# One 32x32 TensorE tile per head for state times queries, two PSUM banks for the attention output, no block-diagonal state, and a new program order

## The reference

```python
x = x + 0.5 * ffn(layernorm(x))
x = x + retention_layer(layernorm(x))
x = x + 0.5 * ffn(layernorm(x))

def ffn(x):                         # x_prev: x shifted by one token
    xr = mu_r * x + (1.0 - mu_r) * x_prev
    xk = mu_k * x + (1.0 - mu_k) * x_prev
    return sigmoid(xr @ W_r.T) * (square(relu(xk @ W_k.T)) @ W_v.T)

def step(S, (qc, kc, vc)):          # 8 heads of 32 channels, one chunk of tokens
    attn = einsum('bhid,bhjd->bhij', qc, kc) * D
    o_intra = einsum('bhij,bhje->bhie', attn, vc)
    o_inter = einsum('bhid,bhde->bhie', qc * decay_q, S)
    S_new = decay_s * S + einsum('bhjd,bhje->bhde', kc * decay_k, vc)
    return S_new, o_intra + o_inter
```

## Time and profile before

| | |
|---|---|
| median of 3 runs | 348.6 us (348.55 to 348.75) |
| the profiled execution's own time | 348.72 us |
| its span in the trace | 346.8 us |
| TensorE busy | 325.5 us (94%) |
| VectorE busy | 302.0 us (87%) |
| ScalarE busy | 211.3 us (61%) |
| GpSimd busy | 161.3 us (47%) |

### The profile page before, as it was taken

How to read it: one execution, slowest core, us unless ns; L and a number is a source line. 1 busy time by engine, 2 the same in 40 slices (tenths; PEclk the granted TensorE clock), 3 DMA queues, 4 the chain that set the end, 5 groups by cost and what they waited for, 6 DMA issues and landing times.

```text
span 346.8 us, 10332 instructions
## 1 busy us (share of the span) xinstructions
PE 325.5 (94%) x3861; PEld 312.9 (90%) x3861; DVE 302.0 (87%) x693; ACT 211.3 (61%) x418; POOL 161.3 (47%) x270
## 2 busy tenths in 40 slices
PE   0869999899999999999999999999999999999874
PEld 0759999899999999999999999999999999999864
DVE  3898997999899998989899898989999897898843
ACT  3675557567657657657757757656766657455352
POOL 4384463435627282644727183563736171414140
PEclk9999999999999999999999999999999999999999
DMA  7611010000101020200202020110000000000001
GB/s 259 221 30 28 9 32 2 33 2 10 54 3 62 2 62 2 62 3 2 62 3 62 2 61 2 22 43 32 3 4 30 2 32 2 33 2 32 33 0 60
DMA packets 11664, 12.15 MB, mean 35 GB/s; under 512 B 992, under 2 KB 11232, under 8 KB 11616
## 3 DMA queue, kind: packets, MB, share of 16 engines
q1 hardware_dynamic: 11328, 11.44, 10.4%
q10 hardware_dynamic: 288, 0.07, 0.1%
HBM read 7.31 MB, written 4.19 MB: 33 GB/s over the span
## 4 chain that ended last, share of the span: by engine, by line
PE 84%; DVE 8%; issue 3%; ACT 2%; POOL 1%; DMA 1%; DVEq 0%; ACTq 0%; POOLq 0%
PE bank L903 36%; PE bank L895 24%; PE bank L887 6%; PE bank L973 5%; PE bank L987 5%; PE bank L1000 4%; PE bank L963 2%; PE bank L1010 2%; DVE stats L524 1%; DMA x<-in_x 1%; DVE xrT L551 1%; DVE xk_lo L556 1%; DVE dT L535 1%; DVE xkT L544 1%; ACT xn L294 1%
## 5 line engine op out<-in xcount | busy, mean ns | idle before, releaser
L213 POOL TENSOR_TENSOR xr_lo<-xrT,xr_hi 128x512 fp32r<-128x512 f32 x32 | 54.3, 1697 | 95.0 <-ACT xr_hi L314 93.7
L294 ACT ACTIVATE xn<-x,shift,rstd 128x256 f32<-128x256 f32 x96 | 52.2, 593 | 12.7 <-POOL shift L209 12.7
L222 POOL TENSOR_TENSOR state_bd<-state,mask 128x256 f32<-128x256 f32 x31 | 27.8, 898 | 39.2 <-DVE state L620 37.2
L606 DVE TENSOR_TENSOR attn<-bank,decay 128x512 f32<-128x512 f32 x64 | 40.4, 677 | 1.0 <-PE bank L973 0.6
L895 PE MATMUL bank<-xk_hi,w_hi 128*128 128x256 f32 x128 | 38.3, 299 | 1.9 <-DVE xk_lo L556 1.9
L903 PE MATMUL bank<-w_hi,xr_hi 128*128 128x256 f32 x128 | 39.0, 305 | 0.5 <-POOL xr_lo L213 0.4
L524 DVE BATCH_NORM_STATS2 stats<-x 128x6 f32<-128x256 f32 x96 | 35.7, 413 | 4.2 <-DMA x<-in_x 4.0
L903 PE MATMUL bank<-w_hi,ka_hi 128*128 128x256 f32 x128 | 36.5, 285 | 2.8 <-DVE ka_lo L562 2.8
L887 PE MATMUL bank<-ident,xn 128*128 128x128 f32 x192 | 30.0, 280 | 9.7 <-ACT xn L294 9.7
L202 POOL TENSOR_TENSOR var_eps<-moments,eps 128x2 f32<-128x2 f32 x48 | 20.6, 428 | 38.3 <-DVE moments L528 38.1
L895 PE MATMUL bank<-xa_hi,w_hi 128*128 128x256 f32 x128 | 36.8, 287 | 0.0
(11 more groups left out here) (80 smaller groups left out, 1071.2 us busy)
## 6 DMA issues: line engine op xcount, KB each, us to landing
x<-in_x SPq DMA_DIRECT2D x16, 256.0 KB, 3.0
x_out<-y SPq DMA_DIRECT2D x16, 256.0 KB, 2.6
w_f<-in_w SPq DMA_DIRECT2D x7, 256.0 KB, 5.4
decay<-in_decay SPq DMA_DIRECT2D x1, 512.0 KB, 6.4
decq<-in_decq SPq DMA_DIRECT2D x1, 256.0 KB, 6.0
deck<-in_deck SPq DMA_DIRECT2D x1, 256.0 KB, 6.1
mask<-in_mask SPq DMA_DIRECT2D x1, 128.0 KB, 5.7
ident<-in_ident ACTq DMA_DIRECT2D x1, 64.0 KB, 2.6
```

Source lines behind the costliest of these rows:

```text
L213: pool.tensor_tensor(xr_lo[f][n % 2][:], xrT[f][n % 2][:], xr_hi[f][n % 2][:].bitcast(F32), ALU.subtract).then_inc(xr_lo_ready[f], 1)
L222: pool.tensor_tensor(state_bd[1 - c][:], state[c][:].unsqueeze(2).broadcast_to([P, G, HG, HD]), mask[:], ALU.mult).then_inc(state_bd_ready ...
L294: act.activation(xn[s][n % 2][:, t, :], x[n % len(x)][:, t, :], ACT.Identity, bias=shift[s][n % 2][:, t:t + 1], scale=rstd[s][n % 2][:, t: ...
L606: dve.tensor_tensor(attn[r][:], bank[B_SCORES[r]][:].rearrange("p (g c i) -> p g c i", g=G, c=TILES), decay[:, r, :, :].unsqueeze(2).broad ...
```

## The change

The product of state and queries is done by 16 matmuls per block, one for each head and chunk, each with 32 rows and 32 columns of the array and 128 columns of queries. They read `state_dec`, which DVE writes in any case. `state_bd`, `mask`, its DMA and POOL's `spread_state` go away. Both chunks are now done in one call, `inter(n)`, and so are those of `outer(n)`. Head `r` of group `g` uses array columns and output partitions `(r + g) % 4`, and each group has a PSUM bank of its own (banks 3 and 4). The rows of Wo are permuted on the host to fit. As `inter` now reads the decayed state of both chunks, it waits for `state_scaled[0]` and `state_scaled[1]`, and DVE's chain from `outer` through `update_state(0)` and `scale_state(1)` stands ahead of it. The banks of nearly everything else are given out anew, and the order of the calls is new on all four engines, with some work moved: the high parts of W_R, W_O and W_VAL are made by POOL, the low part of W_K by DVE. At the start there are 8 and 10 matmuls of keep_warm, in the epilogue none.

```diff
@@ TensorE helpers
-            def inter(c, n):
-                if c == 0:
-                    pe.wait_ge(q_ready, n + 1)
-                    pe.wait_ge(state_bd_ready[0], n)
-                    if n == 0:
-                        pe.wait_ge(state_zeroed, 2)
-                else:
-                    pe.wait_ge(state_bd_ready[1], n + 1)
-                for g in range(G):
-                    mm = pe.matmul(halves(B_OT)[:, g, c * P:(c + 1) * P], state_bd[c][:, g, :, :].rearrange("p h e -> p (h e)"),
-                                   qT[:, g, c * P:(c + 1) * P], start=(c == 0 and g == 0), stop=(c == 1),
-                                   skip_group_check=True)
-                mm.then_inc(inter_done[c], 1)
+            def quadrant(g, r):
+
+                q = (r + g) % HG
+                return slice(q * HD, (q + 1) * HD)
+
+            def inter(n, first=False):
+
+                pe.wait_ge(q_ready, n + 1)
+                for c in range(TILES):
+                    pe.wait_ge(state_scaled[c], n + 1)
+                for c in range(TILES):
+                    for g in range(G):
+                        for r in range(HG):
+                            rows = slice(r * HD, (r + 1) * HD)
+                            mm = pe.matmul(bank[B_OT + g][quadrant(g, r), c * P:(c + 1) * P], state_dec[c][rows, g, :],
+                                           qT[rows, g, c * P:(c + 1) * P], start=(first and c == 0), stop=(not first and c == 1),
+                                           skip_group_check=True)
+                mm.then_inc(inter_done, 1)
@@ POOL
-            def spread_state(c, n):
...
-                pool.wait_ge(state_ready[c], n + 1)
-                pool.wait_ge(inter_done[1 - c], n + c)
-                pool.tensor_tensor(state_bd[1 - c][:], state[c][:].unsqueeze(2).broadcast_to([P, G, HG, HD]),
-                                   mask[:], ALU.mult).then_inc(state_bd_ready[1 - c], 1)
...
             inverse_std(FFN1, 0)
-            split_low(pool, W_K)
+            split_high(pool, W_R)
             inverse_std(FFN1, 1)
@@ TensorE, start
             transpose_T(FFN1, 0)
             pe.wait_ge(w_hi_ready[W_K], 1)
-            keep_warm(3, 8)
+            keep_warm(4, 8)
             pe.wait_ge(xnT_ready[FFN1], 1)
             transpose_T(FFN1, 1)
-            keep_warm(3, 5)
+            keep_warm(4, 10)
             hidden(FFN1, 0, 0)
             hidden(FFN1, 0, 1)
+            pe.wait_ge(xnT_ready[FFN1], 2)
+            transpose_T(FFN1, 2)
             gate(FFN1, 0, 0)
@@ TensorE, epilogue
             retention_out(15, 0)
             retention_out(15, 1)
...
             hidden(FFN2, 14, 0)
             hidden(FFN2, 14, 1)
-            keep_warm(6, 24)
```

More of the change, by code:

```diff
@@ new lines, in _ @@
+                pe.wait_ge(relu_ready[FFN2], i - 4)
+                pe.wait_ge(key_ready, i - 2)
+                pe.wait_ge(xout_ready[RET], i - 3)
+                scores(i - 3, 0, first=True)
+                scores(i - 3, 3)
+                scores(i - 3, 1)
+                scores(i - 3, 2, last=True)
+            pe.wait_ge(krow_ready, 13)
+            outer(12)
+            pe.wait_ge(relu_ready[FFN1], 15)
+            gate(FFN2, 10, 0)
+            pe.wait_ge(val_ready, 13)
+            transpose_T(FFN2, 11)
@@ new lines, in _ @@
+            gate(FFN2, 10, 1)
+            pe.wait_ge(attn_ready[1], 13)
+            gate(FFN1, 14, 0)
+            pe.wait_ge(attn_ready[2], 13)
+            transpose_T(RET, 13)
+            pe.wait_ge(attn_ready[3], 13)
+            pe.wait_ge(o_lo_ready, 12)
+            inter(12, first=True)
+            gate(FFN1, 14, 1)
+            intra(12)
+            pe.wait_ge(gate_ready[FFN2], 11)
+            ffn_out(FFN2, 10, 0)
+            pe.wait_ge(xa_lo_ready, 14)
+            key(13, 0)
+            pe.wait_ge(xnT_ready[FFN2], 12)
@@ new lines, in _ @@
+            pe.wait_ge(krow_ready, 14)
+            outer(13)
+            pe.wait_ge(relu_ready[FFN1], 16)
+            gate(FFN2, 11, 0)
+            pe.wait_ge(val_ready, 14)
+            transpose_T(FFN2, 12)
+            gate(FFN2, 11, 1)
+            pe.wait_ge(attn_ready[1], 14)
+            gate(FFN1, 15, 0)
+            pe.wait_ge(attn_ready[2], 14)
+            transpose_T(RET, 14)
+            pe.wait_ge(attn_ready[3], 14)
+            pe.wait_ge(o_lo_ready, 13)
+            inter(13, first=True)
@@ new lines, in _ @@
+            key_rows(14)
+            pe.wait_ge(gated[FFN1], 16)
+            pe.wait_ge(relu_ready[FFN2], 13)
+            pe.wait_ge(key_ready, 15)
+            pe.wait_ge(xout_ready[RET], 14)
+            scores(14, 0, first=True)
+            scores(14, 2)
+            scores(14, 3)
+            scores(14, 1, last=True)
+            pe.wait_ge(krow_ready, 15)
+            outer(14)
+            pe.wait_ge(gate_ready[FFN2], 13)
+            ffn_out(FFN2, 12, 0)
+            pe.wait_ge(val_ready, 15)
@@ new lines, in _ @@
+            transpose_T(FFN2, 13)
+            pe.wait_ge(attn_ready[2], 15)
+            transpose_T(RET, 15)
+            pe.wait_ge(attn_ready[3], 15)
+            pe.wait_ge(o_lo_ready, 14)
+            inter(14, first=True)
+            ffn_out(FFN2, 12, 1)
+            intra(14)
+            pe.wait_ge(xa_lo_ready, 16)
+            key(15, 0)
+            pe.wait_ge(xnT_ready[FFN2], 14)
+            query(15, 0)
+            key(15, 1)
+            pe.wait_ge(o_lo_ready, 15)
+            retention_out(14, 0)
@@ L1342, in _ @@
+            scores(15, 2, first=True)
+            scores(15, 0)
+            scores(15, 1)
+            scores(15, 3, last=True)
+            pe.wait_ge(krow_ready, 16)
+            outer(15)
+            pe.wait_ge(val_ready, 16)
+            transpose_T(FFN2, 14)
             pe.wait_ge(gated[FFN2], 13)
-            query(15, 0)
+            gate(FFN2, 13, 0)
+            pe.wait_ge(attn_ready[3], 16)
             pe.wait_ge(o_lo_ready, 15)
-            key(15, 0)
-            pe.wait_ge(xout_ready[RET], 15)
@@ L1362, in _ @@
[L1362 to L1370 removed]
+            inter(15, first=True)
+            gate(FFN2, 13, 1)
+            intra(15)
+            pe.wait_ge(gate_ready[FFN2], 14)
             ffn_out(FFN2, 13, 0)
[L1372 removed]
```

981 lines of the change are left out of this document (424 added, 557 removed).

## The result

The changed kernel takes 346.06 us (median of 8 runs, 344.46 to 348.3), the kernel before 348.61 (8 runs, 348.52 to 348.8). The ratio is 0.9928, 95% interval 0.99 to 0.9956: faster by 2.5 us, where 6.8 were forecast. One thing stands out before any trace is opened. The kernel before repeats within 0.3 us, the changed one scatters over 3.8 us, and its times go, roughly, with the mean clock granted to TensorE: 344.46 and 344.77 at 1.00, 345.48 to 347.15 at 0.995, 346.37 and 346.73 at 0.99, 348.3 at 0.985. The profiled execution is the one of 346.37, with a span of 344.6.

The account below looks back on a forecast made before the run. PE's own work bounds the loop, DVE close behind; at the ends, chains between engines. Span 346.8 - 5.0 (`inter`) - 0.7 (start) - 1.1 (end) = 340.0; with 1.9 around it 341.9, median 341.8 us; range 339.3 to 348.5.

Parts of the forecast that it names:

- W: Time of the 32 small `inter` matmuls per block: taken as 0.50 us, bounds 0.44 to 1.10.
- 12 x 0.31: Loop's middle, scores of block 3 to block 15: each block 0.31 us shorter through `inter`, -3.7 us.
- rival 2: Only four small `inter` tiles work at once, 0.90 us per block: 348.2 us, range 346 to 350, chance 0.16.
- The bill of the changes of tiling: PE's cost when matmul shape changes: 0.09 us for emptying, another 0.10 on the way back to full size.
- DVE's and the cover's steps: In the loop, DVE's 18.36 us stays hidden under PE's 19.43; `inter`'s new wait is covered with 1.0 us spare.
- Rival 4: DVE becomes the loop's bound at 19.9 us a period, PE waiting at `inter` or `outer`: 348.9, up to 351; chance 0.10.
- rival 3: Four `inter` tiles at once with weight loads that show, 1.10 us per block: 351.4 us, slower; chance 0.07.
- The end's term of -1.1: Last block: two ffn_out halves cover PE's 1.09 us wait for o_lo, gaining 1.1 us.
- rival 5: Eight tiles overlap, but the clock falls to 1.2 GHz in the end's gap: 343 to 347 us, chance 0.05.
- The start's term of -0.7: Start: denser PE work outweighs a later first hidden matmul, gain 0.7 us, between a gain of 1.8 and loss of 2.0.
- The walk through the start's lists: Walking four engines' lists: some 2.2 us of waits, first query at about 27.5 us with 1.4 us more work done.
- rival 1: The forecast itself: eight small `inter` tiles overlap, 339.5 to 344 us, chance 0.62.

Follow-up runs that it names:

- Run 3: The run 1 kernel without the rotation, so both groups use the four diagonal tiles and W_O's rows are not rotated: 350.97 us, ratio 1.0061.
- run 7: The run 4 kernel with intra directly behind inter in blocks 2 to 13, the gate half behind both: 341.02 us, ratio 0.9771.
- run 1: The changed kernel with the old 24 matmuls of keep_warm put back ahead of the last transposes: 344.72 us, ratio 0.9887.
- Run 6: The run 4 kernel with a gate half (block 13) ahead of the transposes of block 14 in the last block: 345.15 us, ratio 0.989.
- run 4: The run 1 kernel with the FFN2 transposes one gate half later in the loop's first pass only: 344.2 us, ratio 0.9878.
- run 8: The run 4 kernel with POOL's first two steps swapped, the second block's statistics ahead of the W_R copy: 344.13 us, ratio 0.9858.
- run 9: The run 7 kernel with the start's old order of two ACT and DVE steps, and 12 instead of 8 first keep_warm matmuls: 340.65 us, ratio 0.9755.
- run 2: The kernel before without its 24 keep_warm matmuls ahead of the last transposes, nothing else: 349.20 us, ratio 1.0015.
- 10: The run 9 kernel with intra directly behind inter in blocks 1, 14 and 15 too: 341.8 us, ratio 0.9791.

## Why the prediction was wrong in size

**W, "the number that decides", was right.** 0.50 taken, 0.51 measured; the middle stretch gave 12 x 0.294 where 12 x 0.31 was said, the period 19.45 where 19.43 was. Run 3 shows why: with the same four tiles twice W is 0.92, the 0.90 of rival 2. The bill of the changes of tiling (0.09 and 0.10) was right as well: run 7 rests on it.

**DVE's and the cover's steps were right.** PE doesn't wait in the period, at `inter` or elsewhere, not even at 19.19 in run 7. Rival 4 didn't come, nor rival 3.

**The end's term of -1.1 was a wrong step, in two parts.** The wait for o_lo went nearly as the term said, from 1.09 to 0.20. The first part is the clock. The prediction named what was unknown ("what the clock does then isn't in the trace"), bounded it, and then took nothing for it in the sum, with a chance of 0.05 for the clock's fall. It fell in the profiled execution, for 2.3 us (run 1), and in six of eight runs by the clock's mean; in the median it is 1.3. So rival 5 was the case that happened. That its range of 343 to 347 holds the result is in good part luck: its own mechanism gives 341.8 + 1.3 = 343.1, and the rest comes from terms that it had as the forecast had them. The second part is 0.7 us: with the clock up the last stretch is 28.6 (run 1) and not 27.9. Ahead of retention_out it gained 0.9 in place of 1.4, since 0.20 of the wait for o_lo are left and PE idles 0.35 at the transposes of block 14, a wait that the prediction didn't look for. From retention_out to the last transposes it takes 6.64 in place of 6.42, where the prediction said the same chain; 0.17 of these 0.22 are POOL's rstd, 0.86 in place of 0.69. Run 6 shows that the wait at block 14 isn't removed by filling it with the next piece of work.

**The start's term of -0.7 was the other wrong step.** It said a gain. Without the 3 x 0.31 of `inter`, the stretch to scores(3) lost 0.6 in the profile (-0.29 + 0.93), and more in the median. The walk through the start's lists was near: first hidden 13.78 (14 to 15 said), first query 28.28 with two halves more done (27.5 said). It stopped there. A wait of 1.07 from start to start stands at 69.4, where the loop's first pass meets ACT's lists of the ramp, and run 4 gets back 0.4 of it. And the new start scatters: four profiled executions with the same PE list up to there have the scores of block 0 at 32.5 (changed kernel), 33.2 (run 1), 33.9 (run 6) and 33.6 (run 8). The scores of block 3 stand at 86.9 in the kernel before and at 86.6 to 87.6 in these, with the 0.4 of run 4 already in runs 6 and 8. Where it is late, x of the second block landed late (run 8), and in some executions the first hidden also ran at 1.2 GHz (rows under run 9). The kernel before had 5.9 us of standing still in that part, which may take up such scatter. That isn't shown: in both profiles of the old order (the kernel before and run 2) that x had landed by 5.4.

**The account of the median.** 346.06 is 4.3 above the forecast: 1.3 for the clock (346.06 less 344.72 of run 1) and 2.9 between run 1 and 341.8. Of these 0.7 are the end's order, 0.2 at most the middle, and some 2.0 are left for the start, by subtraction; in run 1's own profile it is 2.3. So in the median start and end missed by about as much, 2.0 each. The runs reach from 344.46 to 348.3, all above the 344 up to which rival 1 went. What stays open is why the landing of x differs from one execution to the next, how the later landing and the 1.07 at 69.4 share the start's loss, and what parts the 0.3% between the periods of run 4 and run 1. One remark of the prediction on W does not hold either: a figure for 16 tiles doesn't put eight below 3.5 / 8 = 0.44.

Run 9 beats both kernels: 8.0 us below the kernel before, 5.4 below the changed one. Of that, by the medians, keep_warm gives 1.3, the run with the adjacent tilings 3.2 (2.4 of it in the trace's middle stretch), and the edits of the ramp and the start 0.9, the last two smaller than the scatter of the runs that they are taken from.

## What to carry to other kernels

A new order of the program is to be checked at its two ends as closely as in the loop: an idle stretch of PE whose filler was removed changed the price of the matmuls behind it, at 0.21 us in place of 0.12 here, and a part of that price is hidden where PE waits anyway (run 2). Give an unknown of that kind its own chance by how it would look, not by the absence of a row.

Small tiles pay when different tiles are in flight: count how many distinct tiles the consecutive records use, and put pieces of small tiling next to each other, since each return to the full size costs 0.2 us here.

A wait that is filled with other work is only gone if that work is ready earlier, and if no in-order queue of another engine has its result ahead of what the end hangs on (runs 6 and 10).

## What the runs showed of the hardware

- Eight fp32 tiles of 32x32 at once: 32 records of 128 columns in 0.51 us, 0.016 each; on four tiles 0.92, 0.029 each, as four column strips before (0.028). In both cases both groups write to the same partitions, in two banks.
- The granted clock fell to 1.2 GHz 0.9 us after the matmuls had begun again (idle to 327.69, fall at 328.59), not in the gap: the first full-size matmuls behind the gap still ran 0.12 apart. It came back at 335.42. In run 2 the gap ended at 332.28 and the fall came at 333.89. The Trainium skill, page "TensorE: Matmul & The Clock Gate", Part 1, says that the low level is the default and activity lifts it. These traces agree in that the level fell behind a gap of 3.84 us (start to start) in one and 3.73 in the other, and not where 24 matmuls filled the gap. Behind these nearly equal gaps the low level lasted 6.83 us in the one program and 3.41 in the other.
- At the start the clock column of a stretch is no witness: run 7's matmuls from 15.43 to 16.7 are 0.21 apart, the spacing of 1.2 GHz, under a column of 1.00. There the spacing is the witness.

```profile
15.05:16.89 1.84, 1.84 (x8) 1.84 (x9) 1.76 (x2) 1.12 (x4) 1.31 (x1) 1.00 0.00 0
```
